# Gate scores out of the qkv product, scatters in four parts, and the gate's exponential on ScalarE: a fused attention and mixture-of-experts block

## The chip, the cores and the metric

One core of a Trainium2 chip runs the whole kernel in one launch. The metric is the device time of that core in microseconds. Five engines run their own instruction streams and meet at semaphores: PE (TensorE, matrix products into PSUM), DVE (VectorE), ACT (ScalarE), POOL (GpSimd) and SP (SyncE, which here only issues DMAs).

## The reference

The input is an image x of 192 channels and 128 x 128 pixels. It is normalised over channels, goes through an attention over channels and then through a mixture of four experts of which each pixel (token) uses two.

```python
x = x + conv_ref(_ln_c(x), ...)     # layer norm; qkv = einsum(xn, w_qkv); 3x3 depthwise conv;
                                    # scores over channels (8 heads); softmax; proj
t = _to_tokens(x)                   # 16384 tokens of 192
t = t + ffn_ref(_ln_t(t), ...)

# ffn_ref
scores = einsum('bsd,de->bse', x, gate_w) + gate_b      # 4 scores of each token
probs = softmax(scores);  keep the best two, renormalised (masked)
h = gelu(einsum('bsd,edh->ebsh', x, w1) + b1)           # hidden 768, exact gelu
y = einsum('ebsh,ehd->ebsd', h, w2) + b2
out = einsum('bse,ebsd->bsd', masked, y)
```

## The kernel before, in words

The program has three blocks, one after the other.

**First block: a loop over 32 steps of 4 image rows (512 pixels).** In step i PE transposes the normalised tokens `tn` into channels (L745), multiplies them by `w_qkv` in five tiles of output channels (`z`, L736; weights and data are split in a high and a low part, so each tile is five products), does the first taps of the depthwise convolution as products with diagonal matrices (`dw`, L694), transposes and multiplies q and k for the channel scores (L710, L722), and transposes the raw image of step i + 2 into tokens (L767, L768). Beside each of these four token tiles stand two products with `gwc`, the centred gate weights (L769, L770): they give the four gate scores of the raw x, columns 192 to 195 of `xtok`, which has `CX` = 196 columns. DVE does the rest of the taps (L587), the normalisation `tn` (L613) and the statistics; its tap 0 of channel tile 2 waits for `dw(n, 2)`, which PE issues after the transposes of the raw image. ACT evicts PSUM, POOL adds the last tap and computes the inverse deviations. Steps 3 to 26 are a hardware loop; in five other steps ACT, POOL and SP also split w1 in high and low pieces and store them (L548). `xtok` and v go to DRAM scratch.

**Second block:** the softmax of the channel scores, folded with the projection into one matrix `mt`, and the convolution of v as products with banded matrices.

**Third block: 95 beats.** Tables say what each beat holds: `proj_at` a projection step (4 rows of v times `mt`, plus x, into `x1`, L1781 and L1434; then moments L1441 and L1448, the inverse deviation on POOL L1354 and L1356, the normalised tokens `xn` L1458), `gate_at` a gate batch of four projection steps, `block_at` an expert block of 512 sorted tokens, `comb_at` a step that gathers the two expert outputs of its tokens (L1347) and adds them (L1664). Projection step s is normalised on DVE two beats after its own. The gate of a batch comes three beats after its last projection. The 32 steps form four groups of 8, 12, 8 and 4; the expert blocks of a group need all its tokens. The first 12 beats have no expert block.

A gate batch goes: DVE adds `sraw` and the bias, takes the maximum and subtracts it; POOL raises `e_base` (the number e) to that power (L1360); DVE compares, counts and masks, PE makes the prefix sums (L1791), and DVE turns them into row numbers `idx` (L1566). Then POOL scatters the batch's 16 token tiles to their experts' rows: 32 indirect DMAs (L1334), each with one token a partition. They leave from `xn`, a ring of `XN` = 6 steps, so `normalise(s)` must wait until step s - 6 has left. The semaphore for that counts whole batches:

```python
if s >= XN:
    old = (s - XN) // BATCH
    dve.wait_ge(st_sc[old % 2], 2 * NT * 16 * (old // 2 + 1))
```

POOL's own order in a beat is written out: the inverse deviation of the step one beat back, the exponent of the gate one beat ahead, the scatter of the gate one beat back, the gathers of the combination one beat ahead. In an expert block's beat there are six chunks k of 128 hidden units. PE does `first(J, k)` (five products, L1733) and `second(J, k - 2)` (L1749, L1750), ACT a Gelu (L1382) and a Copy (L1385), DVE the low part `hl` (L1703). PE's `first` of chunk k needs the Gelu of chunk k - 2, and `second` of a chunk needs its `hl`.

Of the kernel before, what the change touches and what calls it, by code (L numbers as in the profile page):

```python
# [17 lines left out]
FP32 = mybir.dt.float32  # L18
F32R = mybir.dt.float32r
# [14 lines left out]
E = 4  # L34
# [15 lines left out]
CX = C + E  # L50
CD = 2 * CA
# [8 lines left out]
E_BASE = 2.718281828459045  # L60
# [56 lines left out]
def build(nc, x, spat, ln_w, ln_b, w_qkv, w_dw, w_proj, temperature, gate_w, gate_b, w1, b1, w2, b2, out):  # L117
    top = ExitStack()
    with top:
# [7 lines left out]
        xtok_dram = nc.dram_tensor("xtok_scratch", (H, W, CX), FP32, kind="Internal").ap()  # L127
# [14 lines left out]
        mt = sb(top, "mt", [G2, 2, CX])  # L142
# [19 lines left out]
        with p1:  # L162
# [4 lines left out]
            xtok = sb(p1, "xtok", [128, 2, ROWS, CX])  # L167
            stat = sb(p1, "stat", [128, 2, ROWS, 6])
            mv = sb(p1, "mv", [128, 2, ROWS, 2])
            rstd = sb(p1, "rstd", [128, 2, ROWS])  # L170
# [13 lines left out]
            wq_ah = sb(p1, "wq_ah", [CA, 3 * C], F32R)  # L184
            wq_al = sb(p1, "wq_al", [CA, 3 * C], F32R)
            wq_ch = sb(p1, "wq_ch", [128, 3 * C], F32R)
            wq_cl = sb(p1, "wq_cl", [128, 3 * C], F32R)
# [9 lines left out]
            zv = sb(p1, "zv", [G2, 2, TOK])  # L197
# [11 lines left out]
            gw_t, gw_ok = sem("gw_t"), sem("gw_ok")  # L209
# [60 lines left out]
            def _(sp):  # L270
# [18 lines left out]
                sp.dma_start(gw[0:CB, 1, :], gate_w[CA:C, :]).then_inc(ld_gw, 16)  # L289
# [46 lines left out]
                def step(i):  # L336
# [14 lines left out]
                    if i.within(0, NB - 1):  # L351
                        sp.wait_ge(z_a, 5 * i.val + 5)
                        for g in (0, 1):
                            sp.dma_start(v_view[:, g, bass.ds(i.val * ROWS + 1, ROWS), :],
                                         zv[:, g, :].rearrange("p (r w) -> p r w", w=W)).then_inc(st_v, 16)
# [11 lines left out]
                sp.wait_ge(st_v, 32 * NB)  # L367
# [5 lines left out]
            def _(pool):  # L373
# [7 lines left out]
                pool.wait_ge(const, 7)  # L381
# [5 lines left out]
                pool.wait_ge(const, 11)  # L387
# [6 lines left out]
                pool.wait_ge(const, 13)  # L394
# [5 lines left out]
                def step(i):  # L400
# [15 lines left out]
                    if b.within(0, NB - 1):  # L416
# [17 lines left out]
                        if not (b.static and b.val < 2):  # L434
                            pool.wait_ge(tn_ok, b.val - 1)
                        nc.gpsimd.tensor_tensor(rstd[:, b.par, :], t[2], t[1], ALU.mult).then_inc(r_ok, 1)
# [16 lines left out]
            def _(act):  # L453
# [8 lines left out]
                def copy_z(i, ct):  # L462
                    c = 5 * i.val + ct
                    m = ZT[ct][1]
# [7 lines left out]
                    else:  # L472
                        if ct == QK:
                            wait(act, st_v, 32 * i.val)
                        nc.scalar.activation(zv[:, ct - QK, :], zb[(i.par + ct) % 2][0:m, :], ACT.Identity,
# [12 lines left out]
                def step(i):  # L488
# [31 lines left out]
                    if b.within(0, NB - 1):  # L520
                        for k in (0, 1):
                            act.wait_ge(xt_t, b.val + 1)
                            if k == 0:
# [3 lines left out]
                                                 tp[k][:, 0:2 * CX].rearrange("p (r c) -> p r c", c=CX),  # L527
# [22 lines left out]
                def setup():  # L550

                    for ct, (o, m) in enumerate(ZT):
# [8 lines left out]
                    act.wait_ge(const, 7)  # L561
# [1292 lines left out]
```

## Time and profile before

| what | us |
|---|---|
| median of 3 runs | 2749.46 |
| lowest, highest | 2746.75, 2766.07 |
| the profiled execution, its own time | 2743.53 |
| its span in the trace | 2741.8 |
| PE busy | 2217.7 (81%) |
| DVE busy | 1559.9 (57%) |
| ACT busy | 1218.6 (44%) |
| POOL busy | 1127.3 (41%) |

The profiled execution is one of the faster ones: 1.7 us outside its span, and 5.9 us under the median. The shares are means over blocks with different limits; the first block runs to about 880 us, the second to about 1050 us.

### The profile page before, as it was taken

The numbers are of one execution on the slowest core, as the hardware profiler recorded it, in microseconds if no ns is written. First come the engines' busy times: TensorE is split into PE (matmuls) and PEld (weight loads), VectorE is DVE, ScalarE is ACT, GpSimd is POOL, SyncE is SP. The second block draws the span as 40 slices with busy tenths as digits, with TensorE's granted clock in tenths as the row PEclk, the third lists the DMA queues.
The fourth block names the chain that finished last, engine by engine and source line by source line (L and its number), as shares of the span: only waits on it lengthen the run. The fifth ranks groups of instructions, "written<-read, shape, count | busy, mean of one in ns | idle before, by whom it ended". The sixth has DMA issues, their size and how long they took to land.

```text
span 2741.8 us, 37767 instructions
## 1 busy us (share of the span) xinstructions
PE 2217.7 (81%) x11436; PEld 1816.1 (66%) x11436; DVE 1559.9 (57%) x3284; ACT 1218.6 (44%) x2129; POOL 1127.3 (41%) x1161
## 2 busy tenths in 40 slices
PE   6599999999585885019957899954999995899993
PEld 5377777777353444019956789953898994799992
DVE  3488898888493334225734646633654563565652
ACT  2355555555353441014523445532565553466661
POOL 2455555555354323640255330356510016543334
PEclk9788888989697998559978899977999997899996
DMA  7432222222412566256655376546664656677763
GB/s 98 88 81 71 63 69 69 64 63 64 86 53 69 151 157 190 84 172 198 206 169 188 124 259 202 193 144 213 219 201 163 205 167 225 204 247 230 236 201 109
DMA packets 302917, 411.02 MB, mean 150 GB/s; under 512 B 33323, under 2 KB 234283, under 8 KB 302765
## 3 DMA queue, kind: packets, MB, share of 16 engines
q1 hardware_dynamic: 278188, 350.39, 42.3%
q0 software_dynamic: 24576, 58.75, 6.9%
q8 instruction: 77, 1.26, 0.2%
q14 instruction: 76, 0.61, 0.1%
HBM read 265.96 MB, written 143.08 MB: 149 GB/s over the span
## 4 chain that ended last, share of the span: by engine, by line
PE 39%; POOL 13%; issue 6%; DVE 2%; DMA 2%; ACT 0%; POOLq 0%; DVEq 0%; SPq 0%
PE bank L1733 16%; PE bank L1749 11%; POOL xs_scratch L1334 9%; PE bank L1750 5%; PE bank L1774 2%; PE bank L1781 2%; POOL yg L1347 2%; PE bank L1755 1%; POOL rt L1360 1%; DMA yg<-y_scratch,ydx 1%; DMA xs_scratch<-xn,idx 1%; PE bank L1797 0%; PE bank L1800 0%; DVE xn L1458 0%; DVE fin L1664 0%
## 5 line engine op out<-in xcount | busy, mean ns | idle before, releaser
L1749 PE MATMUL bank<-w_hl,hh 128*128 x1824 | 552.7, 359 | 172.1 <-DVE hl L1703 170.2
L1703 DVE TENSOR_TENSOR hl<-hf,hh 128x512 fp32r<-128x512 f32 x456 | 314.7, 690 | 375.7 <-ACT hh L1385 375.3
L1382 ACT ACTIVATE hf<-bank,w1b 128x512 f32<-128x512 f32 x456 | 313.9, 688 | 472.2 <-PE bank L1733 472.2
L1749 PEld LDWEIGHTS bank<-w_hl,hh 128*128 128x128 f32 x1824 | 346.5, 190 | 195.4 <-issue 174.9
L1750 PE MATMUL bank<-w_hl,hl 128*128 x1824 | 460.1, 252 | 0.0
L587 DVE SCALAR_TENSOR_TENSOR acc<-zwin,wdw,acc 128x512 f32<-128x512 f32 (+2 forms) x462 | 396.4, 876 | 6.5
L1750 PEld LDWEIGHTS bank<-w_hl,hl 128*128 128x128 f32 x1824 | 351.0, 192 | 19.6
L1347 POOL DMA_INDIRECT yg<-y_scratch,ydx x256 | 249.9, 976 | 270.4 <-DVE fin L1664 119.7
L1733 PE MATMUL bank<-p2xh_a,w1b 128*128 128x512 f32 x912 | 310.2, 421 | 2.1 <-DVE p2x_c L1697 2.1
L1334 POOL DMA_INDIRECT xs_scratch<-xn,idx x256 | 251.4, 982 | 123.1 <-issue 75.8
L1385 ACT ACTIVATE hh<-hf 128x512 fp32r<-128x512 f32 x456 | 288.5, 633 | 14.6
L1733 PE MATMUL bank<-p2x_c,w1b 128*128 128x512 f32 x912 | 288.2, 398 | 0.0
L410 POOL TENSOR_TENSOR last_tap<-acc,last_tap 128x512 f32<-128x512 f32 (+2 forms) x99 | 129.9, 1312 | 311.9 <-DVE acc L587 298.0
L1354 POOL TENSOR_TENSOR rstd<-mv,pw 128x4 f32<-128x4 f32 x32 | 7.4, 231 | 596.8 <-DVE mv L1448 596.8
L694 PE MATMUL bank<-zwin,diag 128*128 128x512 f32 (+2 forms) x462 | 205.8, 586 | 9.4 <-issue 9.4
L1733 PEld LDWEIGHTS bank<-p2x_c,w1b 128*128 128x128 f32 x912 | 173.7, 190 | 41.2
L1733 PE MATMUL bank<-p2xl_a,w1b 128*128 128x512 f32 x456 | 181.5, 398 | 0.0
L1650 DVE TENSOR_REDUCE yo<-bank 128x192 f32<-128x384 f32 x304 | 148.3, 550 | 41.4 <-PE bank L1750 41.3
L1664 DVE SCALAR_TENSOR_TENSOR fin<-yg,gwt,fin 128x192 f32<-128x192 f32 x256 | 91.7, 412 | 127.1 <-DMA yg<-y_scratch,ydx 127.1
L460 ACT ACTIVATE qk_tok<-bank 128x384 f32<-128x384 f32 x128 | 62.7, 490 | 224.0 <-PE bank L710 223.9
L1733 PEld LDWEIGHTS bank<-p2xh_a,w1b 128*128 128x128 f32 x912 | 140.3, 193 | 3.1 <-DVE p2x_c L1697 2.5
L694 PEld LDWEIGHTS bank<-zwin,diag 128*128 128x128 f32 x462 | 83.3, 194 | 85.6 <-issue 84.1
(248 smaller groups left out, 3976.3 us busy)
## 6 DMA issues: line engine op xcount, KB each, us to landing
w1b<-w1s_scratch SPq DMA_DIRECT2D x152, 769.5 KB, 4.7
xs<-xs_scratch SPq DMA_DIRECT2D x76, 512.0 KB, 5.6
y_scratch<-yo SPq DMA_DIRECT2D x76, 384.0 KB
zr<-v_scratch SPq DMA_DIRECT2D x256, 60.0 KB, 2.0
xtok_scratch<-xtok SPq DMA_DIRECT2D x32, 392.0 KB, 2.9
xtok<-xtok_scratch SPq DMA_DIRECT2D x32, 392.0 KB, 4.5
v_scratch<-zv SPq DMA_DIRECT2D x64, 192.0 KB, 3.3
vc_scratch<-cv SPq DMA_DIRECT2D x64, 192.0 KB, 2.5
```

The source lines that it names most:

```text
L410: nc.gpsimd.tensor_tensor(last_tap[:, ct, lo:hi, :], acc[:, ct, lo:hi, :], last_tap[:, ct, lo:hi, :], ALU.add).then_inc(lt_p, 1)
L587: nc.vector.scalar_tensor_tensor(out=a, in0=zwin[n.par][:, ct, ky + lo:ky + hi, kx:kx + W], scalar=wdw[:, ct, DVE_TAPS[ct][k]:DVE_TAPS[ct] ...
L694: last = nc.tensor.matmul(db[(n.par + ct) % 2][:, lo * W:hi * W].rearrange("p (r w) -> p r w", w=W), diag[:, ct, k, :], zwin[n.par][:, ct, ...
L1334: nc.gpsimd.indirect_dma_start(xs_dram, bass.IndirectOffsetOnAxis(ap=idx[:, h, b * NT + t:b * NT + t + 1], axis=0), src, None).then_inc(st ...
L1347: nc.gpsimd.indirect_dma_start(yg[:, s % 2, h, t, :], None, y_dram[g], bass.IndirectOffsetOnAxis(ap=ydx[:, h, s * ROWS + t:s * ROWS + t + ...
L1382: nc.scalar.activation(hf[:, k % 3, :], lb[k % 2][:, :], ACT.Gelu, bias=w1b[:, J % 2, k, 512:513].bitcast(FP32)).then_inc(gelu, 1)
L1385: nc.scalar.activation(hh[:, k % 3, :], hf[:, k % 3, :], ACT.Copy).then_inc(hh_ok, 1)
L1650: nc.vector.tensor_reduce(out=yo[:, J % 2, t, :], in_=yb[t][:, 0:2 * C].rearrange("p (h c) -> p c h", h=2), axis=AX, op=ALU.add).then_inc( ...
L1703: nc.vector.tensor_tensor(hl[:, k % 3, :], hf[:, k % 3, :], hh[:, k % 3, :].bitcast(FP32), ALU.subtract).then_inc(hl_ok, 1)
L1733: last = nc.tensor.matmul(lb[k % 2][:, :], w[:, q, :], v[:, J % 2, :], start=(i == 0), stop=(i == 4))
L1749: nc.tensor.matmul(yb[t][:, 0:2 * C], hh[:, k % 3, cols], w, start=(k == 0), stop=False, skip_group_check=True)
L1750: last = nc.tensor.matmul(yb[t][:, 0:C], hl[:, k % 3, cols], w[:, 0:C], start=False, stop=(k == CH - 1), skip_group_check=True)
```

## The change

1. **Raw scores from the qkv product.** `w_qkv`'s transposed split weights get four more columns, the centred gate weights (`wq_ah` and the others have `C3` = 3C + 4 columns; `ZM` makes the fifth tile 100 wide instead of 96). Since `tn` is the raw token less its mean times `rs`, the product gives the raw scores times `rs`. They go with v's second half through `zv` to a new scratch `u_dram`. The products with `gwc` beside the transposes of the raw image are gone, and `xtok` has 192 columns. In the third block the four rows `u` are loaded under v (`vd`, now up to 100 partitions), `mt` gets four more columns (`CY` = 200) that pass them through, and DVE multiplies them by `rinv`, the reciprocal of all inverse deviations `rs_all`, into columns 192 to 195 of `xtok2`, two instructions a step ahead of the four of L1434. The setup of the gate weights moves behind the first transposes.
2. **Scattering in four parts.** `scatter(b)` of a batch that does not end a group is issued as four parts of 8 indirect DMAs (one step of tokens each) in four beats, and `xn`'s ring waits for its own step. The last batch of a group is scattered whole, as before.
3. **The exponential on ScalarE**, in the gate's beat after chunk k = 1, between two Gelus.
4. PE no longer waits for the low part of b2 before its first projection; that subtraction moves to beat 11.

```diff
-        for t in range(ROWS):
-            ...
-            nc.tensor.matmul(tp[t // 2][:, o + C:o + CX], xc_a[:, b.par, cols], gwc[:, 0, :], start=True, stop=False)
-            last = nc.tensor.matmul(tp[t // 2][:, o + C:o + CX], xc_b[:, b.par, cols], gwc[0:CB, 1, :], start=False, stop=True)
+            last = nc.tensor.transpose(tp[t // 2][:, o + CA:o + C], xc_b[:, b.par, cols], ident[0:CB, 0:CB])
 ...
+                        sp.dma_start(u_dram[:, bass.ds(i.val * TOK, TOK)], zv[G2:G2 + E, 1, :]).then_inc(st_v, 16)
 ...
+                    sp.dma_start(vd[G2:G2 + E, s % 2, 1, :, :].rearrange("e r w -> e (r w)"), u_dram[:, s * TOK:s * TOK + TOK]).then_inc(ld_v[s % 2], 16)
 ...
-                for n in range(n_beats):
-                    b = at(gate_at, n + 1)
-                    if b is not None:
-                        exponent(b)
+                    for part in range(4):
+                        b = at(gate_at, n - 1 - part)
+                        if b is not None and b not in last_batch:
+                            scatter(b, part, 4)
                     b = at(gate_at, n - 1)
-                    if b is not None:
-                        scatter(b)
+                    if b in last_batch:
+                        scatter(b, 0, 1)
 ...
+                        if k == 1 and gate_at[n] is not None:
+                            act.wait_ge(ex_in, gate_at[n] + 1)
+                            nc.scalar.activation(rt[:, 2, :, :], rt[:, 1, :, :], ACT.Exp).then_inc(ex_ok, 1)
 ...
+                    for h in (0, 1):
+                        dve.wait_ge(co_t, 2 * s + h + 1)
+                        ...
+                        nc.vector.tensor_tensor(xtok2[:, s % 2, 2 * h:2 * h + 2, C:CX],
+                                                mb[h][:, 0:2 * CY].rearrange("p (t c) -> p t c", c=CY)[:, :, CX:CY],
+                                                rinv[:, tiles, None].to_broadcast([128, 2, E]), ALU.mult).then_inc(u_ok, 1)
+                    dve.wait_ge(u_ok, 2 * s + 2)
 ...
-                        old = (s - XN) // BATCH
-                        dve.wait_ge(st_sc[old % 2], 2 * NT * 16 * (old // 2 + 1))
+                        dve.wait_ge(st_sc[s % XN], PER_STEP * (s // XN))
```

On PE, in the body of the first block's loop, the transposes of the raw image were followed tile by tile by the two products with `gwc` (here the last two of four tiles, then the transposes of q and k):

```order
214 L767 MATMUL bank<-ident,xc_a 128x128
215 L768 MATMUL bank<-ident,xc_b 128x64
216 L769 MATMUL bank<-gwc,xc_a 128x4
217 L770 MATMUL bank<-gwc,xc_b 128x4
218 L710 MATMUL bank<-ident,qs 128x128 x3
```

```order
168 L772 MATMUL bank<-ident,xc_a 128x128
169 L773 MATMUL bank<-ident,xc_b 128x64
170 L717 MATMUL bank<-ident,qs 128x128 x3
171 L729 MATMUL bank<-qk_tok 96x96 x2
172 L102 ISA
```

The eight products with `gwc` of a step are gone from PE; nothing else of the loop body has moved.

On POOL, in beats 17 to 21 of the third block, around the scatter of batch 2, one exponent, the inverse deviations and the scatter stood so:

```order
342 L1360 TENSOR_TENSOR rt<-e_base,rt 128x64
343 L1354 TENSOR_TENSOR rstd<-mv,pw 128x4
344 L1356 TENSOR_TENSOR rstd<-rstd,pw 128x4
345 L1354 TENSOR_TENSOR rstd<-mv,pw 128x4
346 L1356 TENSOR_TENSOR rstd<-rstd,pw 128x4
347 L1334 DMA xs_scratch<-xn,idx 75264x256 x32
348 L1354 TENSOR_TENSOR rstd<-mv,pw 128x4
```

```order
344 L1363 TENSOR_TENSOR rstd<-mv,pw 128x4
345 L1365 TENSOR_TENSOR rstd<-rstd,pw 128x4
346 L1343 DMA xs_scratch<-xn,idx 75264x256 x8
347 L1363 TENSOR_TENSOR rstd<-mv,pw 128x4
348 L1365 TENSOR_TENSOR rstd<-rstd,pw 128x4
349 L1343 DMA xs_scratch<-xn,idx 75264x256 x8
350 L1363 TENSOR_TENSOR rstd<-mv,pw 128x4
```

The 32 issues in one piece have become pieces of 8 with one step's inverse deviation ahead of each, and the exponent is gone from POOL.

On ACT, in the first gate beat that holds an expert block, a Gelu and Copy of chunk 1 were followed at once by those of chunk 2:

```order
479 L1382 ACTIVATE hf<-bank,w1b 128x512
480 L1385 ACTIVATE hh<-hf 128x512
481 L1382 ACTIVATE hf<-bank,w1b 128x512
482 L1385 ACTIVATE hh<-hf 128x512
483 L1382 ACTIVATE hf<-bank,w1b 128x512
```

```order
495 L1388 ACTIVATE hf<-bank,w1b 128x512
496 L1391 ACTIVATE hh<-hf 128x512
497 L1411 ACT_TABLE_LOAD
498 L1411 ACTIVATE rt<-rt 128x64
499 L1388 ACT_TABLE_LOAD
500 L1388 ACTIVATE hf<-bank,w1b 128x512
```

Two table loads and the Exp stand between chunk 1 and chunk 2 now, in six beats; the Exps of batches 0 and 1 come before the first Gelu and need no load.

## Rows read from the trace of the kernel before

**Rows 1.** The page's chain by line, and whole-run waits: who waited, total us, times, longest.

```profile
PE bank L1733 16%; PE bank L1749 11%; POOL xs_scratch L1334 9%; PE bank L1750 5%; PE bank L1774 2%; PE bank L1781 2%; POOL yg L1347 2%; PE bank L1755 1%; POOL rt L1360 1%; DMA yg<-y_scratch,ydx 1%; DMA xs_scratch<-xn,idx 1%; PE bank L1797 0%; PE bank L1800 0%; DVE xn L1458 0%; DVE fin L1664 0%
...
PE bank L1749 <- DVE hl L1703: 170.2, 5, 40.5
...
DVE xn L1458 <- DMA xs_scratch<-xn,idx: 138.7, 4, 40.6
DVE fin L1664 <- DMA yg<-y_scratch,ydx: 127.1, 8, 43.8
...
PE bank L767 <- issue: 45.6, 3, 15.7
```

**Rows 2.** 16 steps of the loop: busy PE, PEld, DVE, ACT, POOL, then PEclk.

```profile
265.69:620.06 354.37, 354.37 (x1587) 254.41 (x1586) 314.58 (x513) 191.28 (x386) 200.91 (x208) 0.88 0.22 65
```

**Rows 3.** Waits in two steps of the loop, 265.69 to 310.01 us.

```profile
DVE acc L587 <- PE bank L694: 4.6, 4, 2.3
```

**Rows 4.** The same 16 steps, lines L769 and L770 alone: busy PE, PEld.

```profile
265.69:620.06 354.37, 25.93 (x128) 20.33 (x128) 0.88 0.22 65
...
265.69:620.06 354.37, 26.52 (x128) 20.93 (x128) 0.88 0.22 65
```

**Rows 5.** PE's timeline in one step: start us, us.

```profile
315.12 0.39 PE L769 MATMUL bank<-gwc,xc_a 128*128 128x4 f32 x2
...
315.75 0.33 PE L767 MATMUL bank<-ident,xc_a 128*128 128x128 f32 x1
...
318.38 0.58 PE L769 MATMUL bank<-gwc,xc_a 128*128 128x4 f32 x2
...
319.41 0.90 PE L710 MATMUL bank<-ident,qs 128*128 128x128 f32 x3
```

**Rows 6.** Windows of 2 us around it, columns as in Rows 2.

```profile
315.00:317.00 2.00, 2.00 (x12) 1.65 (x12) 2.00 (x4) 1.09 (x2) 1.69 (x5) 1.00 0.87 214
...
319.00:321.00 2.00, 2.00 (x10) 1.98 (x11) 1.97 (x2) 0.58 (x2) 1.55 (x2) 0.50 0.12 17
```

**Rows 7.** POOL's timeline in the first 12 beats (in brackets idle before, releaser).

```profile
1084.36 10.55 POOL L1360 TENSOR_TENSOR rt<-e_base,rt 128x64 f32<-128x64 f32 x1
...
1107.17 1.24 POOL L1334 DMA_INDIRECT xs_scratch<-xn,idx  x1 [0.20 <-issue]
...
1152.06 0.20 POOL L1354 TENSOR_TENSOR rstd<-mv,pw 128x4 f32<-128x4 f32 x1 [4.43 <-DVE mv L1448]
...
1174.17 1.04 POOL L1334 DMA_INDIRECT xs_scratch<-xn,idx  x1 [8.04 <-DVE idx L1566]
```

**Rows 8.** The chain at the end of the first 12 beats: start us, us.

```profile
1213.46 2.39 DMA xs_scratch<-xn,idx
1216.05 3.61 DMA xs<-xs_scratch
```

**Rows 9.** DVE's timeline where it stood idle in the third block.

```profile
1094.94 0.43 DVE L1487 TENSOR_TENSOR cmp<-rt 128x256 f32<-128x256 f32 x1 [6.22 <-POOL rt L1360]
...
1149.17 1.25 DVE L1458 TENSOR_SCALAR xn<-x,mv,rstd 128x192 f32<-128x192 f32 x4 [40.61 <-DMA xs_scratch<-xn,idx]
...
1166.17 0.42 DVE L1487 TENSOR_TENSOR cmp<-rt 128x256 f32<-128x256 f32 x1 [10.66 <-POOL rt L1360]
...
1410.31 1.25 DVE L1458 TENSOR_SCALAR xn<-x,mv,rstd 128x192 f32<-128x192 f32 x4 [32.63 <-DMA xs_scratch<-xn,idx]
```

**Rows 10.** PE and POOL around that last wait, beats 19 and 20.

```profile
1413.84 0.68 PE L1749 MATMUL bank<-w_hl,hh 128*128 x1 [29.75 <-DVE hl L1703]
...
1367.90 1.12 POOL L1334 DMA_INDIRECT xs_scratch<-xn,idx  x1 [0.18 <-ACT xn L1413]
```

**Rows 11.** ACT's one Gelu table load; ACT and PE in the gate beat 18.

```profile
1222.32 1.28 ACT L1382 ACT_TABLE_LOAD   x1
...
1337.33 0.64 ACT L1385 ACTIVATE hh<-hf 128x512 fp32r<-128x512 f32 x1
...
1344.94 0.34 PE L1749 MATMUL bank<-w_hl,hh 128*128 x1
```

More of the change, by code:

```diff
@@ L59 @@
 NEG = -1e30
-E_BASE = 2.718281828459045
 class Step:
@@ L550, in setup @@
                 def setup():
+                    act.wait_ge(gw_ok, 1)
+                    for h, hi in enumerate((wq_ah, wq_ch)):
+                        nc.scalar.activation(hi[:, 3 * C:C3], gwc[:, h, :], ACT.Copy).then_inc(gq_hi, 1)
                     for ct, (o, m) in enumerate(ZT):
@@ L560, in setup @@
                         .then_inc(su_a, 1)
-                    act.wait_ge(const, 7)
+                    act.wait_ge(const, 13)
+                    nc.scalar.activation(mt[G2:G2 + E, 1, CX:CY], ident[G2:G2 + E, G2:G2 + E], ACT.Copy).then_inc(su_a, 1)
                     act.wait_ge(ld_w, 16 * N_LD_W)
@@ L674, in _ @@
             def _(pe):
-                pe.wait_ge(const, 11)
-                pe.wait_ge(ld_gw, 32)
-                nc.tensor.matmul(zb[0][:, 0:E], ones[:, :], gw[:, 0, :], start=True, stop=False)
-                nc.tensor.matmul(zb[0][:, 0:E], ones[0:CB, :], gw[0:CB, 1, :], start=False, stop=True).then_inc(gw_t, 1)
+                pe.wait_ge(const, 9)
                 def dw(n, ct):
@@ L794, in setup @@
                 def setup():
+                    pe.wait_ge(const, 12)
+                    pe.wait_ge(ld_gw, 48)
+                    nc.tensor.matmul(db[0][:, 0:E], ones[:, :], gw[:, 0, :], start=True, stop=False)
+                    nc.tensor.matmul(db[0][:, 0:E], ones[0:CB, :], gw[0:CB, 1, :], start=False, stop=True).then_inc(gw_t, 1)
                     for ct, (o, m) in enumerate(ZT):
@@ L949, in _ @@
                         act.wait_ge(at_t, 3)
-                        nc.scalar.activation(mt[:, :, :], db[0][0:G2, 0:2 * CX].rearrange("p (g o) -> p g o", g=2), ACT.Copy)\
+                        nc.scalar.activation(mt[0:G2, :, 0:CX], db[0][0:G2, 0:2 * CX].rearrange("p (g o) -> p g o", g=2), ACT.Copy)\
                             .then_inc(at_a, 1)
@@ L1172, in chunk_free, with scattered @@
                     eng.wait_ge(y_t, second_done(J - 1, k - 3 + CH))
-            def batches_done(eng, b, upto):
-                for p in (0, 1):
-                    n = (upto + 2 - p) // 2
-                    wait(eng, st_sc[p], 2 * NT * 16 * n)
+            def scattered(eng, upto):
+                for p in range(XN):
+                    wait(eng, st_sc[p], PER_STEP * ((upto + XN - p) // XN))
             def stored(eng, g):
@@ L1323, in _, with scatter @@
                 last.then_inc(c2, 1)
-                def scatter(b):
-                    g = group_of_step[b * BATCH]
+                def scatter(b, part, parts):
                     pool.wait_ge(tn2_dup, BATCH * (b + 1))
                     pool.wait_ge(idx_ok, b + 1)
-                    for t in range(NT):
+                    for t in range(part * NT // parts, (part + 1) * NT // parts):
                         s = b * BATCH + t // ROWS
@@ L1738, in second @@
                     c = CH * J + k
+                    if J == 0 and k == 0:
+                        pe.wait_ge(b2_ok, 1)
                     if k == 0:
@@ L1790, in prefix @@
                     for h, w in enumerate((tri_s, ones)):
-                        last = nc.tensor.matmul(mb[h][:, 2 * CX:2 * CX + NT * E], w[:, :], m, start=fresh, stop=True, skip_group_check=True)
+                        last = nc.tensor.matmul(mb[h][:, 2 * CY:2 * CY + NT * E], w[:, :], m, start=fresh, stop=True, skip_group_check=True)
                     last.then_inc(pf_t, 1)
```

127 lines of the change are left out of this document (67 added, 60 removed).

## The prediction

> **What bounds the kernel now.** I read the chain of waits first: it runs over PE's expert products, and 9% of it lies on POOL's scatter issues [rows 1]. The list of waits names what stops PE. It stood five times for DVE's `hl`, 170.2 us, and DVE in turn stood four times in `normalise` for scatters to leave the ring, 138.7 us [rows 1]. The timeline shows one such pair in beat 20: DVE idle 32.63 us, PE idle 29.75 us [rows 9, 10]. Of the five PE stops three are of this kind (3 x 29.75 = 89). The other two, (170.2 - 89) / 2 = 40.5 each, belong to the gathers that queue on POOL behind the whole scatter of a group's last batch; DVE's `fin` waits 43.8 us there [rows 1].
>
> In the first block's loop PE is busy all 354.37 us of 16 steps, 22.15 us a step, with a granted clock of 0.88; DVE is busy 314.58 / 16 = 19.66 [rows 2] and waits 4.6 / 2 = 2.3 a step for PE's `dw` [rows 3]. So PE bounds the loop and DVE is next, close behind. In the first 12 beats of the third block there are no expert products: DVE and POOL take turns, two powers of 10.55 us and two scatters [rows 7, 9], until the first expert tokens are read at 1216.05 [rows 8].
>
> **The change part by part**, against the profiled execution's 2743.5 us.
>
> *The loop.* A tile's pair of `gwc` products takes 315.75 - 315.12 = 0.63 us, and 319.41 - 318.38 = 1.03 where the clock was at its lower level [rows 5]. Their records are 128 + 128 in 16 steps [rows 4], four pairs a step: 2.5 to 2.9 us, mean 2.7. PE alone would come down to 19.45. DVE without its wait needs 22.15 - 2.3 = 19.85. The larger one rules; the fifth tile's 100 instead of 96 output rows costs PE nothing, as its 512 columns stay, and ACT, busy 191.28 / 16 = 12 us a step [rows 2], has room for four more rows. I take 19.95, 2.2 less a step. In the 26 steps of this length (the 24 of the loop and two beside) that is **-57** (-39 if PE's other waits take a third of it back, -60 at DVE's floor). What is late next is DVE.
>
> *The clock there.* It stood at 1.00 (2.4 GHz) while PE began the raw image's transposes and the four-column products, and at 0.50 (1.2 GHz) right behind them [rows 6]. With that stretch cut the fall may not come. That would lower PE's floor further, and nothing else, as DVE rules.
>
> *Other steps of the first block.* In the five steps with weight pieces PE idles before the same transposes (45.6 us in three of them [rows 1]) and then does them late: between 0 and 4 x 1.03, I take 2.5 each, **-12**. Before the loop two steps' pairs stand on the start-up path at the low clock, 2 x 4 x 1.03 = 8.2; the new setup gives some back and a load of x may come last: **-6** (0 to -10). The store of `u`, one DMA a step, hides behind a DMA share of 0.22 [rows 2].
>
> *First 12 beats.* DVE's stops of 6.22 and 10.66 us for POOL's power [rows 9] become one Exp on an idle ACT, which needs no table load there; I call it 0.5 each. The beats before get two more DVE instructions and a wait for the second half of the projection. Each works on 16 numbers and so stays under the 0.43 us of a 256-wide one [rows 9]: some 0.6 a beat, +4 over seven. PE's dropped wait for b2 gives up to 3 back. So the first scatter starts at 1107.17 - 6.2 + 0.5 + 1 = 1102.5 [rows 7]. An issue takes (1213.46 - 1174.17) / 31 = 1.27 us and the last one lands 2.39 after its start [rows 7, 8]: part 0 has landed at 1115. Step 7's moments and its inverse deviation follow within 4.3 us (from 1149.17 to 1152.06 [rows 7, 9] and the power after it): part 1 runs 1119.3 to 1129.5, parts 2 and 3 to 1149.7. The row numbers of batch 1 are ready before that: `normalise(7)` at 1132, the gate's first steps 2, Exp 0.5, and the 8.0 from 1166.17 to 1174.17 [rows 7, 9] make 1142.6. The whole scatter of batch 1 then lands at 1149.7 + 31 x 1.27 + 2.4 = 1191.4, against 1213.46 + 2.39 = 1215.85: **-24** (-18 to -30). POOL is the bound there, with 64 issues.
>
> *Scatters beside expert blocks.* DVE came to `normalise(14)` at 1410.31 - 32.63 = 1377.7; the scatter had begun at 1367.90 [rows 9, 10]. Part 0 lands at 1367.9 + 10.1 + 2.4 = 1380.4: a wait of 2.7 us in place of 32.6. PE took up 32.63 - 29.75 = 2.9 of a DVE delay, so it should not stop. **-89** for three stops. But eight steps (14 to 19, 26, 27) now meet such a wait, as each part follows the inverse deviation of its beat at the same distance; in beats where DVE also places a batch not all of it is covered. Between 0 and 8 x 2.7 = 22, I take **+3**, near the first end, since 2.7 is under 2.9. After each stop PE ran a product in 0.68 us that takes 0.34 otherwise [rows 10, 11]; three such recoveries go, **-3**. The two stops of 40.5 us stay: those batches scatter whole, and the gathers still queue behind.
>
> *The Exp between Gelus.* A table load took 1.28 us [rows 11], and there are two in each of six beats; the Exp on 64 columns takes less than the Copy of 512, 0.64 [rows 11]. ACT is held up by 2.6 to 3.2 us. The Copy of chunk 1 ended at 1337.97 and PE took chunk 2's product at 1344.94 [rows 11]; Gelu, Copy and `hl` of chunk 2, some 0.64 each, need 1.9 of the 7 between. So 5 us are free: **0**. If ACT does not resume at once after a load the cost is what exceeds 5; I keep 0 to +12 (2 us in each of six beats).
> The Trainium skill speaks against this edit (ScalarE: Activation LUTs, sections "What ACT_TABLE_LOAD costs" and "Table sets: the hidden batching unit"): it wants calls batched by set, and prices a switch at 1283 ns and a drain of 1380 ns. The trace agrees on the load; no run here shows the drain yet. An estimate by it is 5.3 us and the Exp, 5.7, thus 0.7 us over the room in each of six beats, +4 in all.
>
> *Small ones.* The projection has 200 columns instead of 196: 2% of the chain's 2% on L1781 [rows 1], +1. DVE's two instructions in beats with expert blocks hide, as DVE is the idle one there; if that cover were gone, 24 x 0.6 = 14. **+2** for both.
>
> Sum: -57 - 12 - 6 - 24 - 89 + 3 - 3 + 0 + 2 = -186, so 2557.5 for a run like the profiled one. The runs shown lie 3.2 us (lowest) to 5.9 (median) above it; I add 3.5: **2561 us**.
>
> **The rivals.**
> (a) *The loop does not follow*: DVE's wait for `dw` is then not PE's backlog but a chain through ACT's evictions, and only a fifth of 57 comes. For it: PE is never idle in the rows, so how early its inputs are ready can't be seen. Against: DVE's wait is on the product that stands right behind the removed ones. 2561 + 45 = 2606. Chance 0.12.
> (b) *Parts leave too late*: the waits of 2.7 us add up, because a late DVE makes a late inverse deviation and that a late part. Against it: DVE is busy 57% of the run, and in these beats it waits for ACT and can catch up. If nothing is absorbed, +22, and with DVE's extra instructions +14: 2597. Chance 0.12.
> (c) *The change does not do what it says*: `normalise` waits on as before, say because all the queue's descriptors land late together. Then 89 + 15 stay: 2665. The landing 2.39 us after the last issue [rows 8] speaks against it. Chance 0.02.
> (d) *Slower*: PE, no longer always busy in the loop, sits at the 1.2 GHz level throughout. A mean of 0.88 between levels of 1.00 and 0.50 is 76% of the time at the upper one; that part stretches by 1.03 / 0.63: 19.45 x 0.76 x 1.63 + 19.45 x 0.24 = 28.8 us a step, +173 in 26 steps. With the remaining -129 that gives about 2791. It decides from a step of 22.15 + 129 / 26 = 27.1 us. Against it: the stretch before each fall gets shorter, not longer. Chance 0.02.
>
> **How the numbers follow.** The forecast has 0.72; its own range, 2530 to 2590, comes from -40 to -90 in the first block, -18 to -30 in the first beats, and 0 to +34 for the waits and the Exp. Reaching to (a) and (b) gives 2522 to 2612. About 1% (27 us) is what a measurement of this kernel can tell from no change: faster by more 0.95 (the forecast and (a) to (c), less something for what I don't see), within 0.02, slower 0.03 (d and its like).
>
> **What would show it.** After the change the loop's step is near 20 us with DVE without waits for `dw` and PE idle for the first time (right; at 21.5 or more, (a)). The first expert tokens are read some 24 us earlier relative to the block's start. DVE waits in `normalise` seven to nine times, each under 4 us, and PE stands for `hl` twice at 40 us. ACT has 14 table loads, and in the six gate beats PE idles under 1 us each. The prediction is wrong if DVE's instructions in the loop get longer, or if one of the two 40 us stops grows because something new comes ahead of those gathers.

## The result, and the profile after

The changed kernel takes **2623.3 us** (median of four, 2621.1 to 2628.8) against 2748.2 before: 125 us less, where 187 were forecast. The ratio is 0.953, 95% interval 0.949 to 0.958. The profiled execution took 2628.8 us with a span of 2627.1, 114.7 less than the span before. Four stretches hold all of that difference. The first block's last `xh_a` starts at 735.05 instead of 787.84 (52.8 less). The third block's first POOL instruction starts at 999.12 instead of 1049.62 (50.5 less, so the second block gave back 2.3). From there it is 155.4 us to PE's first transposes of expert tokens, the first turn (1154.55), before 170.1 (1219.70): 14.7 less. From that turn to the end are 1472.5 us, before 1522.1 (49.6 less). The forecast had 75, 0, 24 and 87. One execution of a later variant (e17) took 3549 us at a granted clock of 0.56, its other three 2611 to 2613; why is open.

**The loop.** The windows view of 16 steps of the loop, kernel after (its columns are those of [rows 2]):

```profile
249.00:576.00 327.00, 294.79 (x1324) 191.95 (x1323) 315.43 (x511) 188.68 (x383) 208.65 (x208) 0.96 0.24 71
```

Its DVE groups by form (busy us, mean ns), and the waits of DVE and of PE in it:

```profile
L596 DVE SCALAR_TENSOR_TENSOR acc<-zwin,wdw,acc 128x512 f32<-128x512 f32 x224 | 180.2, 822 | 2.8
L622 DVE TENSOR_SCALAR tn<-xtok,mv,rs_all 128x192 f32<-128x192 f32 x64 | 69.2, 1140 | 0.0
```

```profile
DVE acc L596 <- PE bank L701: 8.0, 8, 1.0
...
PE bank L743 <- ACT zwin L474: 27.7, 16, 2.0
PE bank L717 <- POOL qs L420: 4.6, 8, 0.6
```

PE is idle for the first time (32 us of 327) and DVE has next to no wait left. The 24 steps from the fourth `xh_a` on take 20.39 us each (489.4 in all), before 22.12. PE's new wait is for ACT's eviction of z, 1.7 a step; DVE's for `dw` fell to 0.5. But the four `tn` instructions of a step, 0.91 us each in the loop before, now take 1.14 in the mean.

**The first beats.** Two of PE's projections in the timeline of the kernel after, and the windows row of such a beat with the granted clock, 0.50 (in the kernel before four projections in a row took 2.9 us each, at 1.00):

```profile
1019.08 5.70 PE L1801 MATMUL bank<-mt,vd 96*128 96x200 f32 x16 [1.70 <-DVE x L1449]
1026.48 5.70 PE L1801 MATMUL bank<-mt,vd 96*128 96x200 f32 x16 [1.71 <-DVE x L1449]
```

```profile
1018.00:1026.00 8.00, 5.70 (x16) 5.15 (x16) 5.00 (x23) 0.42 (x1) 1.22 (x2) 0.50 0.55 153
```

PE is at the 1.2 GHz level for most of these beats (its first eight projections took 4.4 to 5.7 us), and PE and DVE take turns: 5.70 us of products, 0.17 for the second half of u, 1.41 for the sums: 7.4 a beat. Before, a beat of this kind took 3.8 to 4.2 us. The first scatter therefore starts 62.4 us into the block, where 1102.5 - 1049.6 = 52.9 were forecast; from there to the first turn it is 93.0 us, 92.5 by the forecast's own sum (1191.4 - 1102.5, and the 3.6 by which the turn followed the read before).

**Beside the expert blocks.** The last POOL issue of a part, the DVE instruction that waited for it, and the PE product that waited for DVE, from the timeline after (they answer to [rows 9, 10]):

```profile
1311.91 1.19 POOL L1343 DMA_INDIRECT xs_scratch<-xn,idx  x1 [0.30 <-issue]
...
1319.78 1.25 DVE L1472 TENSOR_SCALAR xn<-x,mv,rstd 128x192 f32<-128x192 f32 x4 [7.51 <-DMA xs_scratch<-xn,idx]
...
1323.31 0.68 PE L1768 MATMUL bank<-w_hl,hh 128*128 x1 [4.59 <-DVE hl L1720]
```

The list of waits after: DVE's of this kind behind the first turn, and PE's from 1160 to 1800.

```profile
DVE xn L1472 <- DMA xs_scratch<-xn,idx: 49.0, 8, 8.1
...
PE bank L1768 <- DVE hl L1720: 28.6, 8, 5.2
PE bank L1793 <- DMA xs<-xs_scratch: 5.6, 1, 5.6
```

Behind such a stop the granted clock falls. The windows row of the 5.8 us behind the one above, and the projection in it, which takes 2.90 us in the beats ahead:

```profile
1323.30:1329.10 5.80, 5.79 (x19) 5.80 (x20) 2.54 (x12) 0.00 (x0) 3.33 (x4) 0.50 0.07 27
...
1325.55 4.67 PE L1801 MATMUL bank<-mt,vd 96*128 96x200 f32 x16
```

The three stops of 29.75 us are gone. In their place `normalise` waits eight times, 3.2 to 8.1 us and 6.1 in the mean, and PE stops behind most of these, 28.6 us in all. The eight beats are together 39.8 us longer than beats of their kind without such a wait; the 11.2 beyond the stops go with the lower clock behind them. The part landed 7.9 us after its last issue began (1311.91 to 1319.78), where the row before had 2.39 [rows 8]. Two PE stops of 39.4 and 39.7 us remain, as forecast.

**The Exp.** ACT's timeline in a gate beat, after:

```profile
1271.69 0.63 ACT L1391 ACTIVATE hh<-hf 128x512 fp32r<-128x512 f32 x1
1272.34 1.28 ACT L1411 ACT_TABLE_LOAD   x1
1273.63 0.26 ACT L1411 ACTIVATE rt<-rt 128x64 f32<-128x64 f32 x1
1273.91 1.28 ACT L1388 ACT_TABLE_LOAD   x1
1275.20 0.69 ACT L1388 ACTIVATE hf<-bank,w1b 128x512 f32<-128x512 f32 x1
```

Each instruction starts 0.01 to 0.02 us after the one ahead of it ends, PE is busy throughout, and there are 14 loads in the run, 1283 ns each.

### The profile page after: what moved, and what is told of

The parts are those of the page before. It is cut to its first block, busy times and chain, and to the rows that moved or that the text cites. A ratio compares the mean times of both kernels' runs of the same rounds, so it can differ in the third digit from the quotient of the medians.

```text
span 2627.1 us, 37195 instructions
## 1 busy us (share of the span) xinstructions
PE 2123.9 (81%) x10924; PEld 1713.7 (65%) x10924; DVE 1570.9 (60%) x3350; ACT 1231.2 (47%) x2152; POOL 1065.1 (41%) x1154
## 4 chain that ended last, share of the span: by engine, by line
PE 41%; POOL 10%; issue 4%; DVE 4%; DMA 3%; ACT 0%; SPq 0%; POOLq 0%; DVEq 0%
PE bank L1750 17%; PE bank L1768 11%; POOL xs_scratch L1343 8%; PE bank L1769 5%; PE bank L1801 3%; PE bank L1793 2%; DMA xs_scratch<-xn,idx 2%; POOL yg L1356 2%; PE bank L1774 1%; DVE xn L1472 1%; PE bank L1817 1%; PE bank L1820 0%; DVE hl L1720 0%; DVE p2xl_a L1713 0%; DVE stat L1456 0%
## 5 line engine op out<-in xcount | busy, mean ns | idle before, releaser
L1768 PE MATMUL bank<-w_hl,hh 128*128 x1824 | 561.1, 362 | 109.6 <-DVE hl L1720 107.7
L596 DVE SCALAR_TENSOR_TENSOR acc<-zwin,wdw,acc 128x512 f32<-128x512 f32 (+2 forms) x462 | 374.8, 829 | 6.6
L1750 PEld LDWEIGHTS bank<-p2x_c,w1b 128*128 128x128 f32 x912 | 173.4, 190 | 41.5
L1793 PE MATMUL bank<-ident,xs 128*128 128x128 f32 x608 | 84.9, 284 | 64.7 <-DMA xs<-xs_scratch 64.7
```

The costliest lines, as they stand in the source:

```text
L596: nc.vector.scalar_tensor_tensor(out=a, in0=zwin[n.par][:, ct, ky + lo:ky + hi, kx:kx + W], scalar=wdw[:, ct, DVE_TAPS[ct][k]:DVE_TAPS[ct] ...
L1750: last = nc.tensor.matmul(lb[k % 2][:, :], w[:, q, :], v[:, J % 2, :], start=(i == 0), stop=(i == 4))
L1768: nc.tensor.matmul(yb[t][:, 0:2 * C], hh[:, k % 3, cols], w, start=(k == 0), stop=False, skip_group_check=True)
L1793: last = nc.tensor.transpose(mb[h][:, t * 128:t * 128 + 128], xs[:, J % 2, t, h * 128:h * 128 + 128], ident[:, :])
```

## Experiments

These runs fell on five chips, by the record, and they are of two kinds. Where e1 to e4 (chip 14), e17 and e18 (chip 13) ran, the kernel before takes 2752 us, about as with the result (kind A). Where e5 to e8 (chip 12), e9 to e12 (chip 0) and e13 to e16 (chip 15) ran, it takes 2865 to 2867 (kind B). Ratios of the two kinds aren't compared; of e5 to e16 the first block and the first beats are, whose lengths agree with those on kind A (20.39 us a step in e9 as in the result).

**One part of the change at a time.** e1 puts the exponential back on GpSimd, e2 the whole scatter, e3 both, so that only the raw scores are left of the change:

```
e1:  +  b = at(gate_at, n + 1)
     +  if b is not None: exponent(b)         # POOL, between inverse_std and the parts
     -  nc.scalar.activation(rt[:, 2], rt[:, 1], ACT.Exp)
e2:  -  for part in range(4): scatter(b, part, 4)
     +  scatter(b, 0, 1);  in normalise: wait for the old batch's last slot
```

> The changed kernel with the gate's exponential again as GpSimd's power, everything else as changed. Theory 'the Exp between Gelus is free' (in the trace of the changed kernel ACT resumes at once after each 1.28 us load and PE never stops there): the power comes back with its own cost alone, DVE waits of some 6 and 10 us in the first 12 beats and one part that leaves 10.6 us later beside the expert blocks, so 2638 to 2655. Rival 'the two table loads in each gate beat cost up to 12 us of the shortfall': then that is given back and the time is 12 us lower than that, 2626 to 2640, with PE's beats at gates visibly shorter than in the changed kernel.

> The changed kernel with each batch scattered whole again and normalise waiting for the whole old batch, everything else as changed. My account of the two traces says that the parts won 50 us beside the expert blocks (three stops of 29.75 less the late parts) and some 17 in the first beats: 2623 + 67 = 2690. The prediction's account says 89 - 3 + 18 = 104: 2727. If something other than the scatter made the shortfall in these beats (the two DVE instructions for u, the Exp), the time lies near 2727 too, as the whole stops come back and that something stays.

> Only the raw scores' part of the change: scatter whole, power on GpSimd. The prediction has -57 -12 -6 in the first block, +4 -3 in the first beats and +2: 2748 - 72 = 2676. My account of the traces has -50.5 for the first block, and the projections that run at the 1.2 GHz level in the first beats, +10: 2748 - 40 = 2708. DVE should be without idle time in the loop except for about 0.5 to 1 us a step, with a step of 20.4.

| kernel | us | ratio to before (95%) |
| --- | --- | --- |
| e3, raw scores alone | 2711.7 | 0.984 (0.981 to 0.987) |
| e2, raw scores and Exp | 2689.0 | 0.976 (0.973 to 0.979) |
| e1, raw scores and parts | 2668.8 | 0.970 (0.967 to 0.973) |
| all three | 2623.3 | 0.953 (0.949 to 0.958) |

e3 and e2 came out within 4 us of my account of the traces, and 36 and 38 us from the forecast's. The three 29.8 us stops are back in e2. e1 was a miss: the power costs 45 us, not 15 to 32. The first turn comes 18 us later in its block (173.4), and behind the turn it is 21 us. There the power can stand ahead of a part, and the wait of that step grows from 4.9 to 13.4 us (timeline of e1). The beats around it lose some 4 us net. Another 17.8 come in one beat: POOL does a power (at 1735.73), then 16 issues of parts and only then the gathers, DVE waits 17.13 us for `yg`, and PE stops for 14.90:

```profile
1362.53 10.55 POOL L1372 TENSOR_TENSOR rt<-e_base,rt 128x64 f32<-128x64 f32 x1 [1.36 <-DVE rt L1503]
1373.26 1.03 POOL L1346 DMA_INDIRECT xs_scratch<-xn,idx  x1 [0.18 <-issue]
...
1384.86 1.25 DVE L1479 TENSOR_SCALAR xn<-x,mv,rstd 128x192 f32<-128x192 f32 x4 [13.41 <-DMA xs_scratch<-xn,idx]
...
1388.39 0.68 PE L1775 MATMUL bank<-w_hl,hh 128*128 x1 [10.49 <-DVE hl L1727]
...
1735.73 10.58 POOL L1372 TENSOR_TENSOR rt<-e_base,rt 128x64 f32<-128x64 f32 x1 [8.94 <-DVE rt L1503]
...
1781.95 0.68 PE L1775 MATMUL bank<-w_hl,hh 128*128 x1 [14.90 <-DVE hl L1727]
```

So the Exp is worth 22.7 us under whole scatters (2711.7 - 2689.0; 15 of them before the first turn), where the stops beside the expert blocks are there anyway, and 45.5 under parts, which need POOL on time. Likewise the parts are worth 43 without it and 66 with it (62 if one goes by the ratios: e1 to e3 did not run beside the result).

**What bounds the loop.** e4 moves ACT's copy of tn behind two of the evictions that followed it. e5 puts it behind all three and DVE's `tn` behind three taps of the third window:

```
e4:  -  for ct in range(2): copy_z(i, ct)
     +  for ct in range(4): copy_z(i, ct)
        act.wait_ge(tn_ok, ...); activation(tn[:, :, C:256], tn[:, :, CA:C], ACT.Copy)
e5:     for t in range(ROWS):
     +      if t == 2: norm()                 # the four tn instructions
            bn_stats(...); tap(n, 2, t + 1)
```

> The changed kernel with ScalarE's copy of tn (which waits for DVE's normalisation) moved behind two of the three evictions of z that follow it, so that PE's wait for them (47.8 us in 28 times in the changed kernel) goes. Theory 'DVE bounds the loop': PE's idle time moves to another wait, the step stays at 20.4, total within 4 us of 2623. Rival 'a chain through ScalarE's evictions bounds the loop, as in rival (a) of the prediction': the step falls by the 1.7 us of PE's wait in each of 28 steps, at best to 19.7, 12 to 20 us faster: 2603 to 2611.

> The changed kernel with DVE's four normalising instructions (tn) moved some 2.5 us later in the step, behind three taps of the third window, where POOL is idle, and ScalarE's copy of tn behind all five evictions of z. Theory 'tn is stretched by POOL's tensor work beside it' (1.14 us each in the changed kernel where the same instruction on 192 elements takes 0.31 to 0.42 in the third block): its mean falls to 0.5 or less, the step to 18.5 to 19.5 as DVE has 2 us less to do, total 2585 to 2605. Rival 'it is long for another reason': mean stays above 0.9, step near 19.9, total 2612 to 2620. Rival 'late tn makes the next image's transposes late': PE waits for the copy of tn, step above 20.

e4: 2615.9 us, 7.4 less than the changed kernel (ratio to before 0.950, 0.947 to 0.953), between the two expectations. The step is 19.94, and the last `xh_a` 7.6 us earlier. So 0.45 of the 20.39 was the chain through ACT's order. The rest is DVE: in e4 it waits for PE only 5.4 us in 327.

In e5 (2742.0 us, kind B) the loop's DVE groups by form, and what PE and DVE wait for there:

```profile
L596 DVE SCALAR_TENSOR_TENSOR acc<-zwin,wdw,acc 128x512 f32<-128x512 f32 x227 | 201.5, 905 | 2.8
L623 DVE TENSOR_SCALAR tn<-xtok,mv,rs_all 128x192 f32<-128x192 f32 x64 | 19.8, 368 | 0.0
```

```profile
PE bank L755 <- ACT tn L547: 33.3, 17, 2.4
DVE acc L596 <- PE bank L704: 31.7, 33, 1.9
```

`tn` falls from 1140 to 368 ns when it runs where POOL is idle. The means hide two values: in the kernel after, the 8 of 64 `tn` with no POOL instruction beside them take 366 to 370 ns, those beside POOL's `qs` 1.34 to 1.45 us; in e5 all 64 take 364 to 370. The `acc` instructions rise from 822 to 905, so some of it only moves: four times 0.77 gained, 14 times 0.08 lost, 1.9 us net. That became a wait: PE waits 2.0 us a step for the late copy of tn and DVE as long for PE; the step is 20.03. The stretch is real and the rival on latency as well. The Trainium skill (SBUF — State Buffer, section "Who interferes with whom") says that VectorE's `tensor_scalar` in a two-port mode and a GpSimd instruction block each other; the rows of `tn` agree, though no run here tells whether it is in such a mode. So the place of such an instruction in the step is a cost, which my floor for DVE took as fixed.

**The clock in the first beats.** e6 lets DVE sum each half of a projection when it is done, so that PE's pause shrinks. e17 keeps the pauses but fills them:

```
e6:  for h in (0, 1):
         dve.wait_ge(co_t, 2 * s + h + 1);  u of half h
     +   dve.wait_ge(u_ok, 2 * s + h + 1);  x1 of tiles 2h, 2h + 1
e17: project(s)
     +   if nxt is None:
     +       for _ in range(4): matmul(lb[0][:, 0:CY], ones[0:G2], mt[0:G2, 0])   # not read
```

> The changed kernel in which DVE adds the tokens of the first half of a projection as soon as that half is done, instead of waiting for both. Theory 'the wait for both halves lets PE pause 1.7 us in each early beat and keeps it at the 1.2 GHz level': the pause falls to about 0.9 us, PE gets to the 2.4 GHz level as before the change (product group 2.9 instead of 5.7 us), and a beat falls from 7.4 to about 4.3 us: 7 beats, 15 to 20 us faster, 2603 to 2608. Rival 'the low level has another cause': the beat falls only by the pause, to 6.6: 4 to 6 us faster, 2617 to 2619. Beside expert blocks nothing in both.

> The changed kernel with four more products (200 columns each, into a bank that nobody reads) behind each projection of the first beats, where PE pauses 1.7 us. Theory 'the pauses keep the level low': PE reaches 2.4 GHz, a projection takes 2.9 to 3.0 us, the beat falls from 7.4 to 4.4 to 5.2, the first scatter comes 12 to 17 us earlier in the block (at +45 to +50 instead of +61). Rival 'the level is not set by these pauses': projections stay at 5.7 us and the beat at 7.4, or above it by what the extra products delay. Beside that no change: total 10 to 15 us below the changed kernel of the same chip, or equal to it.

e6 (2749.4 us, kind B) reached 2.4 GHz: four projections of 2.99, beats of 4.4, the first turn at +143.7 instead of +153.9. Its whole time is that of the changed kernel there (2749.4 too, e9), so these 10 us don't show in it. And e12 and e15 below have the same code in these beats and stayed at 5.70 and 6.75 a beat, with pauses of 1.05 us, shorter than e6's 1.41. Shorter pauses alone don't decide it. e17 fills them (kind A, 2613.0, ratio 0.949, 0.946 to 0.952; its timeline):

```profile
1005.03 5.31 PE L1801 MATMUL bank<-mt,vd 96*128 96x200 f32 x16 [8.62 <-POOL dcon L1332]
1010.18 1.52 PE L1846 MATMUL bank<-mt,ones 96*128 96x200 f32 x8
1012.64 2.96 PE L1801 MATMUL bank<-mt,vd 96*128 96x200 f32 x16 [0.95 <-DMA vd<-u_scratch]
1015.44 1.52 PE L1846 MATMUL bank<-mt,ones 96*128 96x200 f32 x8
1017.30 2.99 PE L1801 MATMUL bank<-mt,vd 96*128 96x200 f32 x16 [0.35 <-DVE x L1449]
```

With the pause cut to 0.35 us by products that nobody reads, the second projection is at the upper level, and so are the next five (also in e18). In the 13 runs with the changed kernel's code in these beats and its pauses of 1.7 us, no projection took less than 4.1. The beat is 4.7, the first turn at +143.9 instead of +155.4, the whole 10 us faster. So the pauses let the level stay low, and the wait for both halves made them.

**The waits of the parts.** e7, e11 and e13 are one kernel, with parts 1 to 3 ahead of the beat's inverse deviation. e8 has a ring of seven slots:

```
e7:  +  for part in range(1, 4): send(at(gate_at, n - 1 - part), part)
        s = at(proj_at, n - LN_D);  inverse_std(s)
     +  send(at(gate_at, n - 1), 0)
e8:  -  XN = 6
     +  XN = 7
```

> The changed kernel with parts 1 to 3 of a batch issued ahead of the beat's inverse deviation, not behind it, so that they leave up to 10 us earlier. Theory 'normalise waits because a part leaves 10 us before it is needed and lands 5 to 8 us after its last issue': six of the eight waits (49 us in all) go, only those for part 0 stay (7.5, 6.3 and 8.0 us); PE gets back some 20 us, and POOL's gaps between parts in the first beats (4 us each) go too: 2590 to 2600. Rival 'a late inverse deviation now holds DVE instead': no gain, 2620 to 2630, with waits of DVE for rstd.

> The changed kernel with a ring of 7 slots for the normalised tokens instead of 6 (room made by reusing other tiles; the pads are then written with half-size descriptors), so each part has a whole beat more to land. Theory as in the run before: no wait in normalise beside expert blocks, PE's stops of 2 to 5 us there go, 28 to 38 us faster: 2585 to 2595. If the lost time beside expert blocks had another source than these waits (the two DVE instructions, the Exp, DMA load), it stays above 2610.

> The changed kernel itself, once more, as the measure for the others of this group: the four runs before this group ran on another chip than the rest (the kernel before took 2865 us there, and PE paused some 2 us at many instructions with no releaser beside the expert blocks), so their ratios can't be set against that of the changed kernel. On a chip like the first one: 2615 to 2630, ratio 0.951 to 0.957. On one like the second: 2745 to 2765.

> The kernel of e7 (parts 1 to 3 ahead of the beat's inverse deviation) beside the changed kernel on the same chip. In e7's trace no wait in normalise was left, and the first expert tokens were read 7 us earlier in the block. Theory 'the late parts cost 28 us beside the expert blocks': 28 to 38 us less than the changed kernel of this group. Rival 'they were only where the delay showed, and PE waits for something else now': within 10 us of it.

> Parts 1 to 3 ahead of the inverse deviation, as in e7 and e11. On a chip where the kernel before takes 2750: 2585 to 2600 (the waits in normalise and PE's stops of 2 to 5 us behind them are the missing part, plus 5 to 7 us in the first beats); 2613 to 2625 if PE's lost time has another source. On one where it takes 2865: 2745 to 2755 as in e11.

All fell on kind B. Times: the changed kernel itself 2749.4 (e9), e7 2748.2, e11 2751.6, e13 2744.5, e8 2737.8. Behind the first turn no wait of DVE for `xs_scratch` over 1 us is left in e7 and e8, and the turn itself comes 4 to 6 us earlier, yet from that turn to the end it is 1594.2 us in e7 and 1596.5 in e9. Other time is lost there. In e9's timeline PE pauses between products of one chunk, for nothing that the profile shows:

```profile
1496.92 0.58 PE L1750 MATMUL bank<-p2xh_a,w1b 128*128 128x512 f32 x1 [1.14 <-issue]
1499.74 0.59 PE L1750 MATMUL bank<-p2xh_a,w1b 128*128 128x512 f32 x1 [2.24 <-issue]
```

The windows view of one whole scatter, 32 issues, in e9, in which PE is busy 16.7 of 41 us:

```profile
1475.73:1516.68 40.95, 16.69 (x74) 12.30 (x73) 9.18 (x29) 4.43 (x7) 31.16 (x32) 0.72 0.63 212
```

Behind the first turn e9 has 50 such pauses of 1.0 to 4.2 us, 115 us in all, and one of 7.3 near the end. All 51 begin in, or up to 5 us behind, the six stretches in which POOL issues 24 to 48 indirect transfers without a break (31 to 62 us), and 47 of them in three of these. Its 28 stretches of 8 or 16 issues have none. All twelve runs on the three chips of kind B have such pauses (34 to 58 a run), and of their 240 stretches of 8 issues only three pauses belong to one. No run on kind A has one, with as many issues.

**The last batches.** e10 and e14 are one kernel: the last batches of groups 2 and 3 leave in eight parts behind the beat's gathers. e12 and e15 add e4's, e6's and e7's edits to it; e16 is e12 with `tn` two taps later (and ACT's copy behind all evictions):

```
e10: -  if b in last_batch: scatter(b, 0, 1)
     +  if b in last_batch[:2]: scatter(b, 0, 1)
        gather(s)
     +  for part in range(8): if b in last_batch[2:]: scatter(b, part, 8)
```

> The changed kernel in which the last batches of groups 2 and 3 leave in eight parts of two tiles each, each part behind the beat's gathers, instead of whole and ahead of them. Theory 'the two PE stops of 40 us stand for gathers queued behind 32 scatter issues on POOL, and the scattered rows are not needed for 10 beats and more': both stops go, as 8 gathers (10.2 us) and 4 issues (5.1 us) fit in a beat of 16.4: 76 to 80 us faster than the changed kernel, some 2545. Rival 'POOL is then late in each of these beats': 16 to 30 us of it come back as DVE waits for yg of 2 to 4 us a beat: 2560 to 2575.

> The changed kernel with four edits: ScalarE's copy of tn behind two more evictions, DVE's sums by halves, parts 1 to 3 ahead of the inverse deviation, the last batches in eight parts behind the gathers. If the terms add up (7 + 11 + 30 + 78): 2623 - 126 = 2497, 9.2% under the kernel before. If the last batches' parts are late (the rival of e10): up to 2525.

> The last batches of groups 2 and 3 in eight parts behind the gathers, as in e10. On a chip where the kernel before takes 2750: both 40 us stops go and little comes back, 2540 to 2560; with POOL late in each of these beats 2560 to 2575. On the other kind 2750 to 2760 as in e10.

> The four edits of e12. On a chip where the kernel before takes 2750: 2497 to 2525. On the other kind 2738 to 2748.

> e12's kernel with DVE's tn two taps later in the step (one less than in e5) and ScalarE's copy of tn behind all evictions. Theory 'POOL's stretch of tn against the latency of tn to the next transposes': tn at some 0.4 to 0.8 us each, the loop's step 19.4 to 19.9 against 19.95, so 0 to 12 us less than e15. Rival 'the latency decides already': step 20.0 or more.

On kind B again: 2756.5 (e10), 2759.3 (e14), 2742.9 (e12), 2739.0 (e15), 2735.0 (e16). The 40 us stops went, but each beat with gathers and a part took 20 to 28 us in e10 instead of 17.5, so the six beats from the stop on took 140 us where e9's took 147 (140 in e14 too; e10's profiled execution lies 17 us above its median). Both also have one pause of 22 us a few beats earlier, for nothing that the profile shows. Spread over stretches of 12 and more issues, the pauses come there too. What this order is worth on kind A was not measured. In e16 `tn` takes 700 ns in the mean, PE waits 1.6 us a step for its copy, and the step is 19.97: the latency decides.

**The version that beats both.** e18 has e16's loop, the sums by halves, e17's filler and the parts first, with the last batches whole:

> e16's kernel without the split of the last batches (which cost on the second chip), with the products of e17. On a chip where the kernel before takes 2865: 2722 to 2735. On one where it takes 2750: 2570 to 2590.

Kind A: **2574.2 us**, ratio 0.935 (0.933 to 0.938), 49 less than the changed kernel, as expected. This run also shows what e7 to e13 could not. From its first turn to the end are 1442.3 us, 30.2 fewer than in the changed kernel and 23.2 fewer than in e17, which ran on the same chip and has the changed kernel's code there (1465.5). DVE's waits for parts, and PE's waits from the turn to the last blocks:

```profile
DVE xn L1478 <- DMA xs_scratch<-xn,idx: 19.0, 3, 6.5
...
PE bank L1774 <- DVE hl L1726: 89.3, 5, 39.7
```

The three waits are those of each batch's part 0; of PE's five stops two are the 40 us ones, the other three 10.2 us together. e18's other edits all act ahead of the first turn, save the sums by halves, which act on two small instructions a beat.

## Why the prediction was wrong

The direction held, and 2623.3 lies above the range (2522 to 2612). By the steps of its sum, from one profiled execution to the other:

| step | forecast | measured | |
| --- | --- | --- | --- |
| 24 of the loop's 26 steps | -53 | -41.6 | DVE's floor right, a wait through ACT on top |
| the other two, piece steps, start-up | -22 | -11.2 | piece steps kept their idle time, a load of x came last |
| second block | 0 | +2.3 | not looked into |
| first 12 beats | -24 | -14.7 | the clock |
| three stops, their residual waits, recoveries, Exp, small ones | -87 | -49.6 | residual waits mis-sized |

**The residual waits** are the step that failed most, 37 of the 71 us. The forecast took +3 for them, "near the first end, since 2.7 is under 2.9", and the eight beats came out 39.8 longer. It put a part's landing at 2.4 us behind its last issue, from [rows 8]. That row is from a moment when PE stood still, with a DMA share of 0.29 (1205 to 1216). In a running beat it is up to 7.9 (with a share of 0.75 from 1312 to 1320), the eight waits have a mean of 6.1 instead of 2.7, and the 2.9 that PE takes up [rows 9, 10] don't cover them. That the load on the queues makes the landing late is likely, but no run varies it alone. The 2.7 was a slip on the safe side: the last of eight issues starts 8.9 us behind the first, not 10.1, so the forecast's own rows give 1.5. A second price was missing: it took 1 us for a recovery and counted only the three that go, but behind the eight new stops the lower clock costs 11.2. Without five of the eight waits 23 to 30 us come back (e18 against e17 and against the changed kernel), so they are most of the missing part. The remaining three beats, 10.6 us too long, and 0.13 us in each beat with a projection (18.23 instead of 18.10) make up most of the rest. Rival (b) had these waits, priced at 22 from the same 2.7; that they add up through late inverse deviations, as it says, is not shown.

**The first beats**: the second half, from first scatter to first turn, was right to 1 us (93.0 against 92.5). What failed is "some 0.6 a beat, +4 over seven" for DVE's two instructions. They cost little themselves (8 numbers each, 0.17 us), but with the wait for both halves PE was mostly at 1.2 GHz. e17's beats of 4.7 us, and its first scatter 11.4 us earlier in the block (at +51.0), show that price.

**The loop**: the step came to 20.39, not 19.95. "Takes a third of it back" was the forecast's own bound for PE's other waits, and 0.45 of 2.2 is what came, through ACT's wait for `tn` (e4: 19.94). This is rival (a) in kind, with a quarter of its price. DVE's instructions did get longer (`tn` 1140 ns for 914: more of them now run beside POOL's `qs`), which the forecast named as a way to be wrong; it was mostly offset by shorter `acc` (822 for 875).

**Start and piece steps**: the first `xh_a` came 9 us earlier, and 5.8 of it went in the next step, where PE waits 14.6 us for x (4.8 before). PE's idle time before the transposes in the piece steps stayed (47.2 us in three, before 45.6); four of these steps got 5.1 us shorter together, where the forecast took 2.5 each.

**Right**: PE no longer bounds the loop; the Exp costs PE nothing. (The Trainium skill, ScalarE: Activation LUTs, section "What ACT_TABLE_LOAD costs", adds a drain of 1380 ns to a load of 1283. The trace shows the 1283 ns and no drain beside them: the load starts 0.02 us behind the Copy, the Exp 0.01 us behind the load.) The three stops of 29.75 go, so rival (c) fell, and the two others stay. What the forecast didn't see is that the Exp and the parts need each other (e1): with the power left on POOL the parts lose 23 of their 66 us. The clock did not hold the loop at 1.2 GHz (granted 0.96, before 0.88), so rival (d) fell.

## What to carry to other kernels

Take a transfer's landing time from a row in which the queues are as loaded as they will be after the change, not from one in which everything waits for that transfer; where a wait is to shrink to a few us, let the transfer be issued ahead of the beat's other work on its engine, not behind it. When a change makes a matrix engine pause, look at the granted clock behind the pause: with pauses of 1.7 us in a short loop a beat took 7.4, and with idle products in the pauses 4.7; stops of 28.6 us in long beats cost 11.2 more. Edits that free the same queue are not additive, so price them as pairs.

## What I had not expected of the hardware

- **Indirect transfers and PE on kind B.** 50 pauses of 1.0 to 4.2 us in PE's stream without a releaser (e9), all in or just behind unbroken stretches of 24 to 48 indirect issues and none at those of 8 or 16; none on kind A with the same program. The kernel before takes 2866 us there and the changed one 2749 (ratio 0.958, 0.955 to 0.961). What makes the pauses is open.
- **A level that stays.** Equal code in the first beats ran four projections in a row at 2.99 us in e6 and e16 and seven at 5.7 in e12 and e15. What brought it to the one or the other is open; filling the pauses gave the upper level both times (e17, e18).
- **A normalising instruction of 192 elements takes 0.37 us or 1.4**, depending on whether POOL's `qs` runs beside it. The means between (368 to 1140 ns) are mixtures of the two.
